# Attention products in 32 bits, the modulation behind the transpose, the gate in the output weights, new orders

## What is computed

```python
mod = (_silu(c) @ wmod).reshape(8, 6, 1, -1)
sa, ca, ga, sb, cb, gb = ...                  # one row of 256 each, per batch
ga = (2 * (ga >= 0) - 1) * jnp.maximum(jnp.abs(ga), 0.25)   # gb likewise
h = _layernorm(x) * (1 + ca) + sa
x = x + ga * attn(h, w_qkv, w_out)            # causal: out_t = q_t kv_t / (q_t ks_t), then @ w_out
h = _layernorm(x) * (1 + cb) + sb
x = x + gb * moe(h)                           # top 2 of 8: cw * (gelu(h w1) w2)
```

## Time and profile before

| | us |
|---|---|
| median of 3 runs | 865.67 |
| lowest and highest | 861.3 and 866.07 |
| the profiled execution, its own time | 863.31 |
| its span on the core | 861.6 |

### The profile page before, as it was taken

How to read it: one execution, slowest core, us unless ns; L and a number is a source line. 1 busy time by engine, 2 the same in 40 slices (tenths; PEclk the granted TensorE clock), 3 DMA queues, 4 the chain that set the end, 5 groups by cost and what they waited for, 6 DMA issues and landing times.

```text
span 861.6 us, 26916 instructions
## 1 busy us (share of the span) xinstructions
PE 713.4 (83%) x8131; PEld 527.0 (61%) x8131; DVE 678.6 (79%) x1491; ACT 605.8 (70%) x1171; POOL 570.3 (66%) x562
## 2 busy tenths in 40 slices
PE   4477778778777877876259999999999999999994
PEld 1245555555555555555147777777777777777773
DVE  3589999998999899895576777777787877777773
ACT  2488888888888888884106777777676777777763
POOL 5457776777777677774484666666676766666652
PEclk7799999999999999997559999999999999999998
DMA  5113342333333332321012433434343433443320
GB/s 199 46 59 121 100 136 80 112 103 109 110 122 110 93 119 87 118 85 47 31 57 55 75 71 69 75 71 75 62 78 71 74 68 73 74 74 67 70 37 1
DMA packets 53840, 70.66 MB, mean 82 GB/s; under 512 B 8984, under 2 KB 44200, under 8 KB 53760
## 3 DMA queue, kind: packets, MB, share of 16 engines
q0 software_dynamic: 18176, 27.06, 17.0%
q1 hardware_dynamic: 35568, 42.45, 15.6%
q10 hardware_dynamic: 16, 0.02, 0.0%
HBM read 48.34 MB, written 22.07 MB: 82 GB/s over the span
## 4 chain that ended last, share of the span: by engine, by line
PE 53%; DVE 19%; issue 9%; POOL 9%; ACT 5%; DMA 3%; SPq 1%; DVEq 1%; another core or an unknown queue 0%; POOLq 0%; ACTq 0%
PE hidden L1354 15%; PE bank L1370 14%; PE hidden L1356 7%; PE bank L1372 7%; DVE w L574 4%; DVE amlo L520 3%; POOL h L812 3%; DVE w1lo_k L574 2%; DMA stage<-in_L_ffn_w_dram 2%; PE bank L1196 2%; PE hidden L1151 2%; PE bank L1102 1%; POOL mod_b L866 1%; PE bank L1104 1%; PE bank L1103 1%
## 5 line engine op out<-in xcount | busy, mean ns | idle before, releaser
L1354 PE MATMUL hidden<-qstT,w1hi_k 128*128 128x256 f16 x1136 | 200.7, 274 | 1.4 <-DVE am L739 1.4
L1356 PE MATMUL hidden<-qstT,w1lo_k 128*128 128x128 f16 x1136 | 195.9, 220 | 0.0
L1370 PE MATMUL bank<-w,amhi 128*128 x568 | 188.6, 379 | 0.6
L1372 PE MATMUL bank<-w,amlo 128*128 x568 | 154.8, 273 | 0.0
L745 DVE TENSOR_TENSOR amlo<-am,amhi 128x512 f16<-128x512 f32 x142 | 98.4, 693 | 62.6 <-ACT am L1090 52.5
L915 POOL DMA_INDIRECT out_dram<-x,si x71 | 118.9, 1675 | 39.9 <-issue 23.9
L1354 PEld LDWEIGHTS hidden<-qstT,w1hi_k 128*128 x1136 | 111.6, 98 | 15.3 <-issue 1.5
L1356 PEld LDWEIGHTS hidden<-qstT,w1lo_k 128*128 x1136 | 111.5, 98 | 1.5
L1089 ACT ACTIVATE amhi<-am 128x512 f16<-128x512 f32 x142 | 88.2, 621 | 15.0 <-DVE am L739 11.2
L1370 PEld LDWEIGHTS bank<-w,amhi 128*128 128x128 f16 x568 | 55.5, 98 | 63.1 <-issue 3.2
L1090 ACT ACTIVATE am<-am 128x512 f32<-128x512 f32 x142 | 87.3, 615 | 0.0
(11 more groups left out here) (223 smaller groups left out, 2011.0 us busy)
## 6 DMA issues: line engine op xcount, KB each, us to landing
stage<-in_L_ffn_w_dram SPq DMA_DIRECT2D x32, 512.0 KB, 3.9
xt<-in_L_attn_x_dram SPq DMA_DIRECT2D x32, 128.0 KB, 2.1
out_dram<-x SPq DMA_DIRECT2D x32, 128.0 KB, 1.7
ffn_rows<-h SPq DMA_DIRECT2D x32, 128.0 KB, 1.7
ffn_rows<-am SPq DMA_DIRECT2D x32, 128.0 KB, 1.7
am<-mod_rows SPq DMA_DIRECT2D x16, 128.0 KB, 3.4
mod_b<-mod_rows SPq DMA_DIRECT2D x8, 256.0 KB, 4.1
am<-mod_rows SPq DMA_DIRECT2D x7, 256.0 KB, 3.8
```

Of the source, the lines that this page charges most:

```text
L1354: t.matmul(dst.rearrange("p (q n) -> p q n", q=2), w1s[0][k][g][:, w_], both, start=(k == 0), stop=False)
L1356: last = t.matmul(dst[:, P:2 * P], w1s[1][k][g][:, w_], both[:, 0, :], start=False, stop=(k == KT - 1))
L1370: t.matmul(y[:, :], ghi[:, m.p, c_m], w2s[mt // 2][:, bass.ds(w_, 2 * D)], start=(mt == 0), stop=False)
L1372: last = t.matmul(y[:, D:2 * D], glo[:, m.p, c_m], w2s[mt // 2][:, bass.ds(w_, D)], start=False, stop=(mt == MT - 1))
```

## The change

1. **First modulation.** `xm` and `h` on POOL are gone, with `mod_a`, the broadcast rows and their loads. `hT` is transposed unmodulated; `hTe` on DVE copies it out of PSUM in two instructions of 128x128, with 1 + ca and sa as numbers per partition (`mod_t`). They are made at the start by 16 small matmuls instead of a product in rows, a copy and a broadcast.
2. **32-bit products.** `wq` and `wo` stay in 32 bits. `v`, `qk` and `pj` are one 32-bit matmul for each 128 rows of the contraction. `hhi`, `hlo`, `ahi`, `alo` and the splitting of the weights at the start are gone; `aTe` (ACT) is one copy.
3. **Gate.** `wb` (POOL) multiplies `wo` by the gate row once a batch (128x512) into `wo_b`; `pj` uses it. `t1` and POOL's `x1` become one DVE instruction, `x1`, which adds the input to the product.
4. **Features.** The high part of k, `shk`, goes to POOL; that of q, `shq`, stays on ACT.
5. **Start.** POOL makes only four constants ahead of the first `rs`; the others follow step 0 and step 2.
6. **Orders.** All five tables are new; `wlo` goes one lag earlier, `so` from lag 5 to 4.

```diff
-ORDER_PE = (("aT", 4), ("ear", 3), ("sc1", 3), ("pj", 4), ("hT", 0), ("h2T", 6), ("pv0", 3), ...
+ORDER_PE = (("aT", 4), ("ear", 3), ("pj", 4), ("sc1", 3), ("hT", 0), ("pv0", 3), ("Tk", 2), ...
-ORDER_POOL = (("rs", 0), ("xm", 0), ("h", 0), ("slo", 2), ("R", 1), ("xm2", 5), ("x1", 4), ("h2", 5))
+ORDER_POOL = (("shk", 2), ("rs", 0), ("slo", 2), ("R", 1), ("xm2", 5), ("h2", 5), ("wb", 2))
-ORDER_ACT = (("exp", 2), ("sh0", 3), ("xn", 0), ("ahi", 4), ("shi", 2), ("sh1", 3), ("xn2", 5), ("hhi", 0),
-             ("whi", 1), ("kTs", 2), ("h2Te", 6), ("vhi", 0), ("sth", 2), ("qTs", 2), ("lge", 6))
+ORDER_ACT = (("exp", 2), ("sh0", 3), ("shq", 2), ("sth", 3), ("aTe", 4), ("whi", 1), ("xn", 0), ("xn2", 5),
+             ("sh1", 3), ("kTs", 2), ("h2Te", 6), ("vhi", 0), ("qTs", 2), ("lge", 6))
-ORDER_SP = (("ldx", 0), ("ld", 2), ("moda", 2), ("modg", 6), ("modb", 7), ("modgb", 6), ("ro", 6), ("gb", 6), ("so", 5))
+ORDER_SP = (("ldx", 0), ("ld", 1), ("ro", 6), ("modgb", 6), ("gb", 6), ("modg", 6), ("modb", 7), ("so", 4))
...
-            def h_rest(m):
-                wait(dve, a_["hhi"], m.n + 1)
-                v.tensor_tensor(hT[:, m.p, 1, :], bank[0][:, 0:D], hT[:, m.p, 0, :], ALU.subtract)\
-                    .then_inc(a_["hlo"], 1)
+            def h_modulated(m):
+                wait(dve, a_["hT"], m.n + 1)
+                wait(dve, a_["qk"], m.n - 1)
+                wait(dve, a_["v"], m.n - 1)
...
+                for k in range(KT):
+                    last = v.tensor_scalar(hT[:, m.p, k * P:(k + 1) * P], bank[0][:, k * P:(k + 1) * P],
+                                           mod_t[:, bass.ds((KT + k) * B + m.b, 1)], mod_t[:, bass.ds(k * B + m.b, 1)],
+                                           ALU.mult, ALU.add)
+                last.then_inc(a_["hTe"], 1)
...
-                v.scalar_tensor_tensor(out=x1[:, m.p, :], in0=bank[2][:, D:2 * D], scalar=1.0 / WS,
-                                       in1=mod_g[:, bass.ds((m.b % 2) * D, D)], op0=ALU.mult, op1=ALU.mult)\
-                    .then_inc(a_["t1"], 1)
+                v.tensor_tensor(x1[:, m.p, :], bank[2][:, D:2 * D], x_slot(m), ALU.add).then_inc(a_["x1"], 1)
...
+                    g.tensor_tensor(wo_b[:, bass.ds((m.b % 2) * KT * D, KT * D)].rearrange("p (k n) -> p k n", k=KT),
+                                    wo[:, :, :], mod_g[:, bass.ds((m.b % 2) * D, D)]
+                                    .rearrange("p (u n) -> p u n", u=1).broadcast_to([P, KT, D]), ALU.mult)\
+                        .then_inc(a_["wb"], 1)
...
+                g.tensor_copy(kst[:, :, 0:2, :], f[:, 1].broadcast_to([P, NH, 2, HD])).then_inc(a_["shk"], 1)
...
-                    last = mm3(dst, xT_[:, 0, c_k], xT_[:, 1, c_k], whi[:, k, n], wlo[:, k, n],
-                               start=(k == 0), stop=(k == KT - 1))
+                    last = t.matmul(dst, xT_[:, k * P:(k + 1) * P], w[k][:, lo], start=(k == 0), stop=(k == KT - 1))
```

More of the change, by code:

```diff
@@ L271, in counters @@
             return {k: sem(prefix + k) for k in names.split()}
-        a_ = counters("a_", "st mv ve rs nb xn xm h hT hhi hlo v vhi vlo qk rope R exp f shi slo Tq qTs Tk kTs"
-                            " state sth stl ear sc0 sh0 sl0 sc1 sh1 sl1 pv0 pv1 den rec at aT ahi alo pj"
-                            " t1 x1 st2 mv2 xn2 xm2 h2 h2T h2Te lg lge whi wlo")
+        a_ = counters("a_", "st mv ve rs nb xn hT hTe v vhi vlo qk rope R exp f shq shk slo Tq qTs Tk kTs"
+                            " state sth stl ear sc0 sh0 sl0 sc1 sh1 sl1 pv0 pv1 den rec at aT aTe pj"
+                            " wb x1 st2 mv2 xn2 xm2 h2 h2T h2Te lg lge whi wlo")
         s_x = [sem(f"s_x{c}") for c in range(CPB)]
-        s_moda = sem("s_moda")
         s_modb = sem("s_modb")
@@ L326, in steps_of, with steps_a @@
             return step
-        def steps_a(eng, step, order, after=None, when=0):
+        def steps_a(eng, step, order, after={}):
             for c in range(2 * CPB):
                 step(At(0, c, CPB))
-                if c == when and after:
-                    after()
+                if c in after:
+                    after[c]()
             with eng.Fori(2, B - 1) as b:
@@ L970, in earlier_done @@
                     wait(act, a_["ear"], (CPB - 1) * prev.b + prev.c)
-            def h_high(m):
-                wait(act, a_["hT"], m.n + 1)
-                wait(act, a_["qk"], m.n - 1)
-                wait(act, a_["v"], m.n - 1)
-                copy(hT[:, m.p, 0, :], bank[0][:, 0:D]).then_inc(a_["hhi"], 1)
-                if isinstance(m.n, int) and m.n == 0:
-                    output_weights()
             def v_high(m):
@@ L1120, in _ @@
             pe.wait_ge(s_ld["wmod0"], 16 * KT)
-            modulation_of(0).then_inc(s_pe, 1)
-            pe.wait_ge(s_dve, marks["mod_a"])
-            t.matmul(bank[7][:, :], batch0, mod_s[0][:, 0:2 * D], start=True, stop=True).then_inc(s_pe, 1)
-            pe.wait_ge(s_pool, POOL_CONST)
+            for q in range(2 * KT):
+                for k in range(KT):
+                    last = t.matmul(bank[1][:, q * B:(q + 1) * B], wmod_raw[k][0][:, q * P:(q + 1) * P], cT[:, k, :],
+                                    start=(k == 0), stop=(k == KT - 1))
+            last.then_inc(s_pe, 1)
             def rest_of_modulation():
+                pe.wait_ge(s_pool, POOL_CONST)
                 pe.wait_ge(s_ld["rw"], 16)
@@ L1263, in a_transpose @@
                 wait(pe, a_["at"], m.n + 1)
-                bank_free(m, ("hlo", 3), ("alo", -1))
+                bank_free(m, ("hTe", 3), ("aTe", -1))
                 transpose_rows(bank[0][:, D:2 * D], attn).then_inc(a_["aT"], 1)
             def projection(m):
-                wait(pe, a_["alo"], m.n + 1)
-                if isinstance(m.n, int) and m.n == 0:
-                    pe.wait_ge(s_dve, marks["wo"])
-                bank_free(m, ("vlo", 3), ("t1", -1))
-                product(bank[2][:, D:2 * D], aT, wohi, wolo, slice(0, D)).then_inc(a_["pj"], 1)
+                wait(pe, a_["aTe"], m.n + 1)
+                if m.c == 0:
+                    wait(pe, a_["wb"], m.b + 1)
+                bank_free(m, ("vlo", 3), ("x1", -1))
+                lo = (m.b % 2) * (KT * D)
+                product(bank[2][:, D:2 * D], aT[:, :], [wo_b[:, bass.ds(lo + k * D, D)] for k in range(KT)], slice(0, D))\
+                    .then_inc(a_["pj"], 1)
             def h2_transpose(m):
                 wait(pe, a_["h2"], m.n + 1)
-                bank_free(m, ("rope", 5), ("lge", -1))
+                bank_free(m, ("rope", 5), ("lge", -1), ("h2Te", -1))
                 transpose_rows(bank[1][:, 0:D], h2[:, m.p, :]).then_inc(a_["h2T"], 1)
```

269 lines of the change are left out of this document (121 added, 148 removed).

## The result

| | us |
|---|---|
| before, median of 4 runs beside the change | 864.11 (861.3 to 866.07) |
| after, median of 4 runs | 825.26 (823.38 to 825.53) |
| ratio, with its 95% interval | 0.9548 (0.9513 to 0.9583) |
| profiled execution of after, span | 825.53, 823.2 |

The gain is 39 us. Where it lies is read from three marks that both traces have: the start of `sl1` for the first tile, for the last, and the end of the span.

The account below looks back on a forecast made before the run. The prediction took DVE, with its turns against POOL, as the attention stage's nearest bound; the expert stage stays. From 863.3 us it took 33 for 31 shorter steps and 6 for the start: 824, range 805 to 846.

Parts of the forecast that it names:

- The step: One attention pipeline step: from 11.37 to 10.3 us, ends 9.6 and 11.0, saving 33 us over 31 steps.
- DVE's busy time: DVE work in one attention step: from 10.43 to 9.5 us.
- The `wlo` pair: Two DVE instructions per attention step: 2.1 us together instead of 2.77, with one POOL instruction against them; ends 1.36 and 2.77.
- `hTe`, +0.56 said: DVE's copy out of PSUM, now two halves at 0.28 us each: +0.56 us per attention step.
- PE, 9.63 said: PE's busy time per attention step: 9.63 us, +0.81 from the 32-bit products, making it the second bound.
- Rival (c): 32-bit weight loads on PE not hidden, each exposed by 0.19 us: step 12.6, slower at 895 us; chance 0.05.
- The waits: DVE's waits in an attention step: 0.94 us before, 0.8 kept, since PE leaves less slack.
- Rival (d): The loop through the attention features is the bound: step 11.2, 852 us; chance 0.12, of which 0.04 no difference.
- The DMA term: DVE's waits in an attention step due to the weight stream: 0.4 us for w1's tiles, said to go.
- The start, -6 said: Before the pipeline fills: first product near 10 instead of 17.43, net 6 us saved (3 to 9).
- The stretch behind the last `sl1`: Everything behind the attention stage, 460 us: unchanged, otherwise the account is beside the point.
- The bounds: Total for attention steps of 10.7 to 10.0 us: 833 to 812 us, given chance 0.52.

Follow-up runs that it names:

- e_nb_pool: The changed kernel with `nb` computed on POOL behind `rs` instead of on DVE: 818.97 us, ratio 0.9474.
- e_half: The changed kernel with the second half of the contraction left out of `v`, `qk` and `pj`: 820.86 us, ratio 0.9513.
- e_old_orders: The changed kernel's works in the lags and sequence of the kernel before: 854.45 us, ratio 0.9940.
- e_shk_act: The changed kernel with `shk` written by ACT as before the change, no copy on POOL: 829.83 us, ratio 0.9599.
- b_sp: The kernel before with SP's stores one step later (`ro` lag 6 to 7, `so` 5 to 6): 860.74 us, ratio 0.9971.
- e_nb_half: The changed kernel with `nb` on POOL and half the contraction left out of `v`, `qk` and `pj`: 816.66 us, ratio 0.9458.
- e_pool_reads: The changed kernel with three extra POOL products of SBUF tensors at the end of each POOL step: 828.46 us, ratio 0.9655.
- e_pool_writes: The changed kernel with five extra POOL fills, which read nothing, at the end of each POOL step: 826.54 us, ratio 0.9627.

## Why the prediction was right, and where it was not

The forecast was 824, the median is 825.26. So near a hit is partly luck: some of its terms were off and made up for each other.

- **The step, 10.3 said, 10.39 measured** (10.50 in the steady part). DVE's busy time was put at 9.5; in the steady part it is 0.965 x 10.50 = 10.13. Waits were put at 0.8; they are 0.37.
- **The `wlo` pair, 2.1 said** (the value with one POOL instruction against it). It is 1.52 in the quoted step, 1.69 in the mean: 0.4 better. The mechanism was right: one meeting instead of two, and it is shorter than the early pair of the earlier trace rows because the last modulation starts before `wlo`.
- **`nb`: not in the sum at all.** This is the step that failed. The prediction had the rule of turns between two-operand DVE instructions and POOL, and used it on the two big ones only. `nb` reads two SBUF tensors and was moved from a silent POOL to stand beside `slo`: 0.155 to 0.941, +0.79 a step, 24 us of DVE's time over the stage. By length it is nothing; a turn costs what is left of POOL's instruction. e_nb_pool showed it: with the turn gone the step is 0.42 shorter. It also shows that the two misses hang together. There DVE reaches `wlo` 7.0 us after `f`, near the 6.9 that the prediction laid out, and the pair takes 2.10, just what it assumed; in after `nb` delays `wlo` to 7.8, and the pair gets its 1.69 by that.
- **`hTe`, +0.56 said.** 407 ns each, 0.73 for the two: each costs as a whole 128x256 copy of the earlier trace rows, the upper end of its bound. +0.17.
- 9.5 - 0.4 + 0.79 + 0.17 = 10.06 of the 10.13: DVE is accounted for to about 0.1, and no better. The 9.5 starts from 10.43, which is the window's share of the mean step of 11.37; for the steady step of 11.51 it was 10.56. And the two splits that went were 0.33 each in the timeline from one start to the next, not 0.42, since neighbours on DVE overlap at their ends.
- **PE, 9.63 said:** 0.920 x 10.50 = 9.66. Rival (c) is out: the four records of `qk` stand in 1.82 us (the rows below, from start to next start) against the 1.72 said, with no idle time before them; with their loads in the open they would have taken 2.5. Nor does PE set the step (e_half). **POOL, 7.1:** 0.670 x 10.50 = 7.03, with `shk` at 0.61 instead of 0.9 and `wb` at 1.73. **ACT, 8.8:** 9.04. PE's rows in the steady part of after:

```profile
206.78 1.98 PE L1189 MATMUL bank<-wq,hT 128*128 128x512 f32 x4
208.60 0.38 PE L1180 MATMUL bank<-ident,attn 128*128 128x128 f32 x2
```

- **The waits.** They were said to be the small change of slack between engines, kept nearly whole. They shrank by 0.6 a step since the new tables set the works so, which no term had. By e_old_orders most of the gain hangs on that: there the works' relief of 0.76 us of DVE turned into 0.70 of waiting.
- **Rival (d)**, the loop through the features, did not come about: in 200 to 300 us of after DVE waited 0.3 us in all, and with `shk` back on ACT (e_shk_act) the step stays at 10.50. The wait of e_old_orders is another one, `x1` for `pj`.
- **The DMA term, 0.4 a step,** was too large: b_sp gave 0.13.
- **The start, -6 said, -4.4 measured.** The first product began at 11.03, not 10: the 16 small matmuls ran until 9.14, the first transposes stood behind them, and the numbers per partition were copied at 9.70. That is 6.4 earlier than before, and 2.0 of it had gone again by the first `sl1`. The rows are those of PE and DVE at the start of after:

```profile
5.59 3.55 PE L1097 MATMUL bank<-w,w 128*128 128x8 f32 x16 [2.02 <-DMA w<-in_L_wmod_dram]
9.00 0.67 PE L1180 MATMUL bank<-ident,h 128*128 128x128 f32 x2
11.03 5.45 PE L1189 MATMUL bank<-wq,hT 128*128 128x256 f32 x8 [1.36 <-DVE hT L475]
```

```profile
9.70 0.38 DVE L464 TENSOR_SCALAR mod_t<-bank 128x16 f32<-128x16 f32 x2 [3.13 <-PE bank L1180]
10.24 0.73 DVE L475 TENSOR_SCALAR hT<-bank,mod_t 128x128 f32<-128x128 f32 x2 [0.16 <-DVE mod_t L464]
```

- **The stretch behind the last `sl1`, unchanged said, -3.5 measured.** 1.9 of it lie ahead of the expert stage's first split (in the first 10 us behind the last `sl1` the granted clock was 0.71 after and 0.50 before), 1.6 in the expert stage, whose traces spread by 3.6 us on kernels that don't differ there. It is not put down to the change.
- **The bounds.** The prediction gives 833 to 812 for a step of 10.7 to 10.0. That takes 9 us for the start; with its own 6 the two are 836 and 815. The measured time lies inside either.

What sets the step now is DVE with its turns (e_half, e_nb_pool), with ACT ruled out by e_shk_act. Why e_nb_half stays at 10.11 with PE relieved was read from busy shares, not shown by a run of its own.

## What to carry to other kernels

Go through every DVE instruction with two SBUF operands, the tiny ones first, and look at what POOL runs when it starts: its price is what is left of POOL's instruction, and moving anything else moves the meeting. Here, with four engines 74 to 92% busy, taking work off them without a new order mostly made DVE wait; run the new works in the old order before crediting the gain to them. Compare such kernels by the steady step as well, not by one profiled span, when the ends of the pipeline can run at either clock.

## What the runs showed of the hardware that was not expected

- A DVE instruction on 128x2 numbers took 0.94 us in the mean beside a POOL instruction of 1.16 and 0.15 without one. `var`, a TENSOR_SCALAR with one SBUF operand and the same shape, was held up as well at times: 0.55 us beside a POOL cast in e_pool_reads (row below) and 0.58 in e_pool_writes, both in the step with `wb`; 0.17 in every other steady step.

```profile
212.71 0.55 DVE L446 TENSOR_SCALAR var<-mv 128x2 f32<-128x2 f32 x1
```

- 128x128 from PSUM with two numbers per partition costs DVE 407 ns, as much as other rows of 128x256 (409 for `x1`).
- A POOL cast of 128x512 takes 609 ns, its difference of two 128x512 operands 1.16 us.
- The granted clock of TensorE fell or stayed in the same few steps of nearly the same kernel, and the steps differed by 3.6 us.
